# Summing the expert bias rows on 8 partitions, and lending their buffer to an eleventh Toeplitz slot

## The chip, the cores and the metric
The program runs on one core of one Trainium2 chip. The metric is the device time of the whole program in microseconds (us), the median of several runs. The kernel is written by hand for each engine: TensorE (PE in the profile), VectorE (DVE), ScalarE (ACT), GpSimd (POOL), and SyncE (SP), which issues most of the DMAs. Every engine runs its own list of instructions in order, and semaphores tie the lists together.

## The reference, cut to what matters
4096 tokens (32 sequences of 128) go through one layer with 256 channels:

```python
h = embed(ids)                                   # four tables, each with a projection to 256
n = layernorm(h)
x = silu(depthwise_conv(n @ w1.T + w1_b))
# state space: 16 states a channel, h = h * sigmoid(A) + x * B ; y = h . C + D * x, along one axis of x
y = ssm(x)
h = h + (y * silu(n @ v1.T + v1_b)) @ w2.T + w2_b
f = layernorm(h)
shared = silu(f @ sw1 + sb1) * (f @ sw3 + sb3) @ sw2 + sb2
# each token goes to two of eight experts, given by its number alone (11 n + 7919 k) mod 8
out = h + (shared + (expert_a(f) + expert_b(f)) / 2) / 2
```

An expert's second product adds its row `b2[e]` (256 numbers). A token of residue class e therefore ends with the constant row `0.5 * sb2 + 0.25 * (b2[e] + b2[e - 1])`, the same on all 128 partitions. There are 8 such rows, and they are what the change computes in another way.

## The kernel before, in words
**Phase A**, from the start to about 122 us, goes over four groups of 8 rows of 128 tokens (`run_phase_a`; the order of tasks in a row is `phase_a`). Per row, POOL gathers embeddings 6 rows ahead, TensorE transposes and projects them, ACT and DVE evacuate each product as a high and a low half, and the row is normalised: DVE `eps` (L1093), POOL `power_pair` (L613, one power -0.5 for two rows), DVE `norm` (L1079). Every finished row is stored by `h_store` (L471 to L475). Between its gathers POOL computes the state kernel (`kernel_step`), writes it to DRAM (L669) and then does `piece_lo(0)` (L675), the low half of a weight, at the head of group 3 (`group`, L677 to L690).

**The state stage**, from about 122 to 150 us, is 16 chunks of 16 channels. Chunk q takes 32 small matmuls (L1344 and L1346) against a Toeplitz matrix that SP loads in two DMAs (`toep_part`, `toep_load`) from the kernel rows in DRAM. The matrices lie in a ring of 10 slots of 8 KB a partition (`TRING`). Chunks 0 to 9 are loaded ahead, in phase A; chunks 10 to 15 are loaded into a slot when the chunk that used it is done (L538 to L540). A slot that is loaded again needs three quarters of the bytes, because its zero corner is there already. From chunk 8 on, each chunk is followed by four transposes (`y_turn`, L1326). ACT and DVE evacuate each half chunk (L918, L1151).

**Behind it** come the product with `w2`, the second layernorm, and eight expert slots of about 31 us each, in which TensorE works without gaps. The first bias row is needed in `mixer_1` (L763), where POOL adds it to the residual (L748).

**The bias rows before.** SP loads `sb2` and the eight rows `b2` to all 128 partitions after row 7 of group 0 (L504, L505). ACT scales them in rows 4 to 7 of group 1 (L848 to L853). POOL waits for half a chunk of the state stage (L712) and then adds them up with 17 chained instructions of 128x256 (L713 to L717). `w2_b` comes to all partitions twice: into `first_row` after all of the Toeplitz loads (L543), and into `w2_bias` when POOL's chain is done (L562).

**SP's order at the end of the stage** is: the reloads of chunks 10 to 15; `first_row`; the first quarter of the residual (`h_load(0, 0)`, L558); three weight pieces (L559); `w2_bias`; and after the last chunk four weight pieces, a residual part, and piece 8 (L563 to L568).

Of the kernel before, what the change touches and what calls it, by code (L numbers as in the profile page):

```python
# [15 lines left out]
F32 = mybir.dt.float32  # L16
# [26 lines left out]
TRING = TRIGHT + TLEFT  # L43
# [52 lines left out]
def _tower(nc, ctx, ids, table, small, rows, w_a, w_b, w_e, kernel_rows, h_rows, out):  # L96
# [6 lines left out]

    R, L = "right", "left"
    v_sb = sb(ctx, "v_sb", [P, HALVES, BATCH * SEQ], F32, R)
    w2_hi = sb(ctx, "w2_hi", [P, HALVES, D], F32R, R)
    w2_lo = sb(ctx, "w2_lo", [P, HALVES, D], F32R, R)
    bias_e = sb(ctx, "bias_e", [P, RES, D], F32, R)
# [43 lines left out]
    x_sil = sb(mem_a, "x_sil", [P, 4, 4, SEQ], F32, L)  # L152
    x_ids = sb(mem_a, "x_ids", [P, GROUPS, RES], I32, L)
# [18 lines left out]
    mem_row = ExitStack()  # L172
    first_row = sb(mem_row, "first_row", [P, 1, D], F32, L)
    mem_row.close()
# [27 lines left out]
    first_row_in = sem("first_row_in")  # L202
# [12 lines left out]
    bias_step = sem("bias_step")  # L215
# [180 lines left out]
    BIAS_STEPS = 1 + 2 * RES  # L396

# [19 lines left out]
    def toep(q):  # L417
        slot = q % TRING
        return toep_r[:, slot, :, :, :, :] if slot < TRIGHT else toep_l[:, slot - TRIGHT, :, :, :, :]
# [47 lines left out]
    def _(sp):  # L467
# [25 lines left out]

        def piece_in(n):
            raw, _, _, signal, _, _, _, src = PIECES[n]
            sp.dma_start(raw, src).then_inc(signal, 16)
# [7 lines left out]
        sp.dma_start(bias_row[:, 0:1, :], bass.AP(rows.tensor, D, [[0, P], [D, 1], [1, D]])).then_inc(rows_in, 16)  # L504
        sp.dma_start(bias_e[:, :, :], bass.AP(rows.tensor, 2 * D, [[0, P], [D, RES], [1, D]])).then_inc(rows_in, 16)  # L505
        for i in range(1, GROUPS - 1):
            for r in range(RES):
                h_store(i, r)
        last = GROUPS - 1
# [27 lines left out]
        toep_load(9)  # L537
        for q in range(TRING, NQ):  # L538
            sp.wait_ge(ssm_done, 2 * (q - TRING + 1))
            toep_load(q)  # L540
            if q == NQ - 1:
                sp.wait_ge(mm_done, 8 * GROUPS)
                sp.dma_start(first_row[:, :, :], bass.AP(rows.tensor, 0, [[0, P], [D, 1], [1, D]])).then_inc(first_row_in, 16)  # L543
# [13 lines left out]
        sp.wait_ge(ssm_done, 2 * (TRING - 3))  # L557
        h_load(0, 0)  # L558
        for n in range(1, 4):  # L559
            piece_in(n)  # L560
        sp.wait_ge(bias_step, BIAS_STEPS)
        sp.dma_start(w2_bias, bass.AP(rows.tensor, 0, [[0, P], [D, 1], [1, D]])).then_inc(rows_in, 16)  # L562
# [5 lines left out]
        piece_in(8)  # L568
        sp.wait_ge(h2_done, GROUPS)
# [20 lines left out]
    def _(pool):  # L590
# [86 lines left out]
        def group(i):  # L677

            for r in range(RES):
                if i == GROUPS - 1 and r == 0:  # L680
                    piece_lo(0)
                if r % 2 == 0 and (r or i):
                    power_pair(RES * i + r - 2, (r - 2) % 4)
                if r + LEAD < RES:
                    gather(i, r + LEAD)
                elif i + 1 < GROUPS:
                    gather(i + 1, r + LEAD - RES)
                if i == 1 and r or i == 2:
                    kernel_step(2 * (RES * (i - 1) + r) - 2)
                    kernel_step(2 * (RES * (i - 1) + r) - 1)  # L690
# [11 lines left out]

        steps = 0

        def link(ins):
            nonlocal steps
            steps += 1
            ins.then_inc(bias_step, 1)
            pool.wait_ge(bias_step, steps)

        pool.wait_ge(bias_scaled, 5)
        pool.wait_ge(ssm_done, 1)  # L712
        link(nc.gpsimd.tensor_copy(bias_row[:, 1, :], bias_e[:, RES - 1, :]))  # L713
        for e in range(RES - 1, -1, -1):
            before = bias_e[:, e - 1, :] if e else bias_row[:, 1, :]
            link(nc.gpsimd.tensor_tensor(bias_e[:, e, :], bias_e[:, e, :], before, ALU.add))
            link(nc.gpsimd.tensor_tensor(bias_e[:, e, :], bias_e[:, e, :], bias_row[:, 0, :], ALU.add))  # L717
        assert steps == BIAS_STEPS

# [31 lines left out]
        def mixer_1():  # L751
# [10 lines left out]
            power_step(GROUPS + 1, 1, eps2_done, rstd2_done)  # L762
            mixer_bias(0, 0, 0)  # L763
# [26 lines left out]
        def add_w2_bias(par, times, g, row=w2_bias):  # L790
# [4 lines left out]
            nc.gpsimd.tensor_tensor(at, at, row[:, 0, :], ALU.add).then_inc(h_biased, 1)  # L795
# [12 lines left out]
        pool.wait_ge(first_row_in, 16)  # L808
        for g in range(GROUPS):
            add_w2_bias(0, 1, g, first_row)  # L810
# [6 lines left out]
        pool.wait_ge(rows_in, 48)  # L817
# [10 lines left out]
    def _(act):  # L828
# [12 lines left out]
        def cat_hi(i, r):  # L841
# [6 lines left out]
            if isinstance(i, int) and i == 1 and r >= 4:  # L848
                if r == 4:
                    act.wait_ge(rows_in, 32)  # L850
                    nc.scalar.mul(bias_row[:, 0, :], bias_row[:, 0, :], 0.5).then_inc(bias_scaled, 1)
                at = bias_e[:, 2 * r - 8:2 * r - 6, :]
                nc.scalar.mul(at, at, 0.25).then_inc(bias_scaled, 1)  # L853
                if r == RES - 1:
                    piece_hi(0)
# [135 lines left out]
    def _(dve):  # L991
# [65 lines left out]
        def cat_lo(i, r):  # L1057
# [4 lines left out]
            if isinstance(i, int) and i == 0:  # L1062
                beside_cat(r)

# [467 lines left out]
```

## Time and profile before
| | |
|---|---|
| median of 3 runs | 422.75 us (422.54 to 425.06) |
| the profiled execution | 423.13 us, of which the span is 421.4 us |
| granted TensorE clock over the span | 0.996 |
| TensorE busy | 398.5 us, 95% of the span |
| weight loads on TensorE | 351.0 us, 83% |
| DVE, ACT, POOL busy | 271.0, 242.8 and 219.8 us |
| DMA | 39.01 MB, 93 GB/s over the span |
| DMA between 90 and 122 us | 309 GB/s, all 16 engines busy |

Busy time tells how long an engine had an instruction in it. TensorE's share is that of a pipelined engine, so the chain of waits and the engine's gaps tell more than the 95%. "Issue" as the cause of a gap means that the profile shows nothing that the engine waited for. Times in the rows are microseconds from the span's start.

### The profile page before, as it was taken

Reading aid. Unit: us, or ns where it says so; the run is one execution under the profiler, and the core shown is the slowest. Engines: PE = TensorE matmul, PEld = TensorE weight load, DVE = VectorE, ACT = ScalarE, POOL = GpSimd, SP = SyncE. Lnnn points to the kernel's source line nnn. Section 1 sums busy time; section 2 is a strip of 40 time slices with the busy share of each in tenths; the row PEclk is TensorE's granted clock in tenths of the full one; section 3 lists DMA queues with packets and bytes.
Section 4 is the critical chain, followed back from the end, with each engine's and each line's share of the span. In section 5 each row is a group of like instructions: output and inputs, shape, how many; then the busy total and the mean of one; then the engine's idle time right before and its main releaser. Section 6 shows DMA issues by size and latency. Waiting matters only on the chain.

```text
span 421.4 us, 8449 instructions
## 1 busy us (share of the span) xinstructions
PE 398.5 (95%) x2895; PEld 351.0 (83%) x2895; DVE 271.0 (64%) x609; ACT 242.8 (58%) x438; POOL 219.8 (52%) x265
## 2 busy tenths in 40 slices
PE   2899999999999898999999999999999999999996
PEld 1888887879778876888988988888888888888886
DVE  6887988879766698975564564554554554554333
ACT  4688978768886356635536536536436436436442
POOL 7788999821028084996346446446446446434000
PEclk9999999999999899999999999999999999999999
DMA  4353111299969971101301301301301301100101
GB/s 114 115 151 109 51 54 54 72 301 312 318 189 267 256 275 57 51 0 52 101 0 51 100 2 51 100 0 50 100 1 50 100 0 50 50 0 0 51 0 51
DMA packets 32924, 39.01 MB, mean 93 GB/s; under 512 B 3477, under 2 KB 29171, under 8 KB 32768
## 3 DMA queue, kind: packets, MB, share of 16 engines
q1 hardware_dynamic: 29760, 33.12, 26.1%
q0 software_dynamic: 3136, 5.52, 4.4%
q8 instruction: 16, 0.26, 0.3%
q14 instruction: 12, 0.10, 0.1%
HBM read 34.69 MB, written 8.65 MB: 103 GB/s over the span
## 4 chain that ended last, share of the span: by engine, by line
PE 74%; DVE 13%; issue 4%; ACT 4%; POOL 2%; DMA 1%; DVEq 0%; ACTq 0%; POOLq 0%
PE ps L1256 22%; PE ps L1258 21%; PE ps L1257 21%; PE ps L1344 3%; PE ps L1388 2%; DVE v_sb L1145 1%; DVE sw_lo L1136 1%; PE ps L1264 1%; DVE stat L1066 1%; PE ps L1297 1%; PE ps L1346 1%; DVE catT_lo L1059 1%; DVE x_mid L1120 1%; PE ps L1326 1%; DVE x_mid L1127 1%
## 5 line engine op out<-in xcount | busy, mean ns | idle before, releaser
L1193 DVE SCALAR_TENSOR_TENSOR hid_lo<-act_out,hid_hi 128x512 fp32r<-128x512 f32 x64 | 48.7, 763 | 55.9 <-ACT hid_hi L952 55.9
L939 ACT ACTIVATE act_out<-ps,vec 128x512 f32<-128x512 f32 x32 | 22.1, 690 | 89.5 <-PE ps L1258 89.5
L1187 DVE SCALAR_TENSOR_TENSOR act_out<-ps,vec,act_out 128x512 f32<-128x512 f32 x32 | 24.0, 750 | 50.7 <-ACT act_out L939 50.7
L748 POOL TENSOR_TENSOR h_sb<-h_sb,bias_e 128x256 f32<-128x256 f32 x32 | 24.5, 770 | 60.8 <-DVE h2n L1079 60.8
L1256 PE MATMUL ps<-h2nT_hi,sw_hi 128*128 128x512 f32 x128 | 50.0, 391 | 0.0
L1257 PE MATMUL ps<-h2nT_lo,sw_hi 128*128 128x512 f32 x128 | 50.0, 391 | 0.0
L1258 PE MATMUL ps<-h2nT_hi,sw_lo 128*128 128x512 f32 x128 | 50.0, 391 | 0.0
L741 POOL TENSOR_TENSOR zc_lo<-v_sb,zc_hi 128x256 fp32r<-128x256 f32 x32 | 29.8, 931 | 26.3 <-ACT zc_hi L929 26.3
L943 ACT ACTIVATE act_out<-ps,vec 128x512 f32<-128x512 f32 x32 | 22.1, 691 | 34.1 <-PE ps L1258 33.9
L606 POOL DMA_INDIRECT cat<-table_dram,x_ids x32 | 36.5, 1142 | 8.5 <-issue 6.2
L952 ACT ACTIVATE hid_hi<-act_out 128x512 fp32r<-128x512 f32 x64 | 39.7, 623 | 0.0
L1256 PE MATMUL ps<-sw_hi,hid_hi 128*128 128x256 f32 x128 | 37.9, 296 | 0.1
L1256 PE MATMUL ps<-ex_hi,hid_hi 128*128 128x256 f32 x128 | 36.9, 288 | 0.4 <-DVE hid_lo L1193 0.4
L1258 PE MATMUL ps<-ex_hi,hid_lo 128*128 128x256 f32 x128 | 36.2, 283 | 0.0
L1257 PE MATMUL ps<-ex_lo,hid_hi 128*128 128x256 f32 x128 | 36.2, 283 | 0.0
L1258 PE MATMUL ps<-sw_hi,hid_lo 128*128 128x256 f32 x128 | 36.1, 282 | 0.0
L1257 PE MATMUL ps<-sw_lo,hid_hi 128*128 128x256 f32 x128 | 36.1, 282 | 0.0
L1256 PE MATMUL ps<-proj_hi,catT_hi 128*128 128x256 f32 x96 | 30.4, 317 | 2.6 <-DVE catT_lo L1059 2.3
L1256 PE MATMUL ps<-hnT,wv_hi 128*128 128x512 f32 (+1 forms) x64 | 27.6, 431 | 1.0 <-ACT x_pad L897 0.5
L1258 PEld LDWEIGHTS ps<-h2nT_hi,sw_lo 128*128 128x128 f32 x128 | 24.0, 188 | 5.1
L1256 PEld LDWEIGHTS ps<-h2nT_hi,sw_hi 128*128 128x128 f32 x128 | 24.2, 189 | 4.1
L1258 PE MATMUL ps<-proj_hi,catT_lo 128*128 128x256 f32 x96 | 27.5, 286 | 0.0
(136 smaller groups left out, 1262.8 us busy)
## 6 DMA issues: line engine op xcount, KB each, us to landing
toep_l<-kernel_rows_dram SPq DMA_DIRECT2D x14, 512.0 KB, 7.3
toep_r<-kernel_rows_dram SPq DMA_DIRECT2D x12, 512.0 KB, 7.4
h_rows_dram<-h_ring SPq DMA_DIRECT2D x32, 128.0 KB, 2.1
h_in<-h_rows_dram SPq DMA_DIRECT2D x8, 512.0 KB, 4.4
stage<-w_e_dram POOLq DMA_DIRECT2D x7, 512.0 KB, 3.6
out_dram<-o_sb SPq DMA_DIRECT2D x7, 512.0 KB, 3.2
bias_e<-rows_dram SPq DMA_DIRECT2D x1, 1024.0 KB
toep_r<-kernel_rows_dram SPq DMA_DIRECT2D x4, 256.0 KB, 6.1
```

The source lines that it names most:

```text
L606: pool.indirect_dma_start(cat[:, r, :], None, table, bass.IndirectOffsetOnAxis(ap=x_ids[:, i, r:r + 1], axis=0), bounds_check=VOCAB - 1, o ...
L741: nc.gpsimd.tensor_tensor(zc_lo[:, g, :, :], z_cols(e, g), f32(zc_hi[:, g, :, :]), ALU.subtract).then_inc(zc_lo_done, 1)
L748: nc.gpsimd.tensor_tensor(at, at, bias_e[:, bass.ds(e, 1), :].rearrange("p o c -> p (o c)"), ALU.add).then_inc(h2_biased, 1)
L939: nc.scalar.activation(act_out[:, n % 4, :], ps[bank][:, :], ACT.Silu, bias=vec[:, C_SB1 + j:C_SB1 + j + 1]).then_inc(act_done, 1)
L943: nc.scalar.activation(act_out[:, n % 4, :], ps[bank][:, :], ACT.Gelu, bias=vec[:, bass.ds(C_B1 + 2 * x + j, 1)]).then_inc(act_done, 1)
L952: nc.scalar.mul(hid_hi[:, n % 4, :], act_out[:, n % 4, :], 0.5 if kind == SHARED else 0.25).then_inc(hid_hi_done, 1)
L1187: nc.vector.scalar_tensor_tensor(act_out[:, n % 4, :], ps[bank + 1][:, :], vec[:, C_SB3 + j:C_SB3 + j + 1], act_out[:, n % 4, :], ALU.add, ...
L1193: nc.vector.scalar_tensor_tensor(hid_lo[:, n % 4, :], act_out[:, n % 4, :], 0.5 if kind == SHARED else 0.25, f32(hid_hi[:, n % 4, :]), ALU ...
L1256: nc.tensor.matmul(out_, hi, rhs_hi, start=start, stop=False, **kw)
L1257: nc.tensor.matmul(out_, hi, rhs_lo, start=False, stop=False, **kw)
L1258: return nc.tensor.matmul(out_, lo, rhs_hi, start=False, stop=stop, **kw)
L1344: nc.tensor.matmul(at, t_hi, x_sb[:, c, :, :].rearrange("u w b -> u (w b)"), start=True, stop=False, skip_group_check=True)
```

## The change
- The ring gets an eleventh slot, `toep_b`, at the address of `bias_e`, which is 8 KB a partition as well. The upper left half of the slot is cleared by POOL in group 3, behind `piece_lo(0)`; its chunk 10 is then loaded with the bytes of a reload, behind chunk 9. Chunks 11 to 15 are reloads. A reload of chunk q now waits for chunk q - 11.
- `sb2` (8 times) and the rows `b2` (once as they are, once shifted by one) are loaded to 8 partitions, in a part of `x_sil` that group 1 does not use yet: four small DMAs in group 1 (`bias_part`). DVE adds them in rows 5 and 6, ACT scales the sum in row 7 (one 8x256 instruction in place of one 128x256 and four 128x512), and SP stores the 8 rows to DRAM.
- `bias_e` is loaded from there to all partitions behind piece 8, after the state stage. POOL waits for it ahead of the first use.
- POOL's 17 instructions, `first_row` and its load, and the later load of `w2_bias` are gone; `w2_bias` is loaded once, in group 1.
- SP loads the first residual part right after its wait for chunk 6, and then waits for all projections ahead of pieces 1 to 3.

```diff
-TRING = TRIGHT + TLEFT
+TRING = TRIGHT + TLEFT + 1
...
+    mem_b = ExitStack()
+    toep_b = sb(mem_b, "toep_b", [P, PAIRS, SEQ, 2, 2], F16, R)
+    mem_b.close()
     bias_e = sb(ctx, "bias_e", [P, RES, D], F32, R)
...
+    b2_at, b2_before = x_sil[0:RES, 3, 0:2, :], x_sil[0:RES, 3, 2:4, :]
+    sb2_rows, bias_rows = x_sil[0:RES, 2, 0:2, :], x_sil[0:RES, 2, 2:4, :]
...
-        sp.dma_start(bias_row[:, 0:1, :], bass.AP(rows.tensor, D, [[0, P], [D, 1], [1, D]])).then_inc(rows_in, 16)
-        sp.dma_start(bias_e[:, :, :], bass.AP(rows.tensor, 2 * D, [[0, P], [D, RES], [1, D]])).then_inc(rows_in, 16)
+        half = [SEQ, 2], [1, SEQ]
         for i in range(1, GROUPS - 1):
             for r in range(RES):
                 h_store(i, r)
+                if i == 1 and r == 0:
+                    bias_part(b2_at, bass.AP(rows.tensor, 2 * D, [[D, RES], *half]))
+                    bias_part(b2_before[1:RES], bass.AP(rows.tensor, 2 * D, [[D, RES - 1], *half]))
+                if i == 1 and r == 1:
+                    bias_part(b2_before[0:1], bass.AP(rows.tensor, (RES + 1) * D, [[D, 1], *half]))
+                    bias_part(sb2_rows, bass.AP(rows.tensor, D, [[0, RES], *half]))
+                if i == 1 and r == 2:
+                    sp.dma_start(w2_bias, bass.AP(rows.tensor, 0, [[0, P], [D, 1], [1, D]])).then_inc(rows_in, 16)
+            if i == 1:
+                sp.wait_ge(bias_scaled, 1)
+                sp.dma_start(h_bias, bias_row[0:RES, 1, :]).then_inc(bias_out, 16)
...
         toep_load(9)
+        sp.wait_ge(top_zero, 1)
+        toep_part(TRING - 1, 0, HALF)
+        toep_part(TRING - 1, 1, 0)
         for q in range(TRING, NQ):
             sp.wait_ge(ssm_done, 2 * (q - TRING + 1))
             toep_load(q)
-            if q == NQ - 1:
-                sp.wait_ge(mm_done, 8 * GROUPS)
-                sp.dma_start(first_row[:, :, :], bass.AP(rows.tensor, 0, [[0, P], [D, 1], [1, D]])).then_inc(first_row_in, 16)
...
-        sp.wait_ge(ssm_done, 2 * (TRING - 3))
+        sp.wait_ge(ssm_done, 2 * 7)
         h_load(0, 0)
+        sp.wait_ge(mm_done, 8 * GROUPS)
         for n in range(1, 4):
             piece_in(n)
-        sp.wait_ge(bias_step, BIAS_STEPS)
-        sp.dma_start(w2_bias, bass.AP(rows.tensor, 0, [[0, P], [D, 1], [1, D]])).then_inc(rows_in, 16)
...
         piece_in(8)
+        sp.wait_ge(bias_out, 16)
+        sp.dma_start(bias_e[:, :, :], bass.AP(h_bias.tensor, 0, [[0, P], [D, RES], [1, D]])).then_inc(bias_in, 16)
...
                 if i == GROUPS - 1 and r == 0:
                     piece_lo(0)
+                    nc.gpsimd.memset(toep_b[:, :, 0:HALF, :, :].rearrange("p j t c w -> p j (t c w)").bitcast(F32),
+                                     0.0).then_inc(top_zero, 1)
...
-        pool.wait_ge(bias_scaled, 5)
-        pool.wait_ge(ssm_done, 1)
-        link(nc.gpsimd.tensor_copy(bias_row[:, 1, :], bias_e[:, RES - 1, :]))
-        for e in range(RES - 1, -1, -1):
-            before = bias_e[:, e - 1, :] if e else bias_row[:, 1, :]
-            link(nc.gpsimd.tensor_tensor(bias_e[:, e, :], bias_e[:, e, :], before, ALU.add))
-            link(nc.gpsimd.tensor_tensor(bias_e[:, e, :], bias_e[:, e, :], bias_row[:, 0, :], ALU.add))
...
+            pool.wait_ge(bias_in, 16)
             mixer_bias(0, 0, 0)
...
-        pool.wait_ge(first_row_in, 16)
+        pool.wait_ge(rows_in, 16)
         for g in range(GROUPS):
-            add_w2_bias(0, 1, g, first_row)
+            add_w2_bias(0, 1, g)
...
             if isinstance(i, int) and i == 1 and r >= 4:
-                if r == 4:
-                    act.wait_ge(rows_in, 32)
-                    nc.scalar.mul(bias_row[:, 0, :], bias_row[:, 0, :], 0.5).then_inc(bias_scaled, 1)
-                at = bias_e[:, 2 * r - 8:2 * r - 6, :]
-                nc.scalar.mul(at, at, 0.25).then_inc(bias_scaled, 1)
+                if r == 7:
+                    act.wait_ge(bias_summed, 2)
+                    nc.scalar.mul(bias_row[0:RES, 1, :].rearrange("p (b t) -> p b t", b=2), bias_rows, 0.5).then_inc(bias_scaled, 1)
...
+            if isinstance(i, int) and i == 1 and r == 5:
+                dve.wait_ge(bias_parts_in, 64)
+                nc.vector.tensor_tensor(b2_at, b2_at, b2_before, ALU.add).then_inc(bias_summed, 1)
+            if isinstance(i, int) and i == 1 and r == 6:
+                dve.wait_ge(bias_summed, 1)
+                nc.vector.scalar_tensor_tensor(bias_rows, b2_at, 0.5, sb2_rows, ALU.mult, ALU.add).then_inc(bias_summed, 1)
```

## Rows read from the trace of the kernel before

**Rows 1.** Chain that ended last, by engine, from the page
```profile
PE 74%; DVE 13%; issue 4%; ACT 4%; POOL 2%; DMA 1%; DVEq 0%; ACTq 0%; POOLq 0%
```
**Rows 2.** TensorE in order of time, chunks 11 to 15: start, us, line, idle before
```profile
139.66 0.19 PE L1344 MATMUL ps<-x_sb,toep_r 128*128 128x64 f16 x1
...
142.31 0.18 PE L1346 MATMUL ps<-x_sb,toep_r 128*128 128x32 f16 x1 [1.45 <-issue]
...
143.19 0.26 PE L1344 MATMUL ps<-x_sb,toep_r 128*128 128x64 f16 x1
...
147.03 0.19 PE L1344 MATMUL ps<-x_sb,toep_l 128*128 128x64 f16 x1
...
148.56 0.19 PE L1344 MATMUL ps<-x_sb,toep_l 128*128 128x64 f16 x1
```
**Rows 3.** Busy us by stretch: PE, PEld, DVE, ACT, POOL, granted clock, DMA share, GB/s
```profile
90.00:103.00 13.00, 13.00 (x90) 11.77 (x89) 10.92 (x26) 10.73 (x21) 1.81 (x2) 1.00 1.04 336
121.50:124.90 3.40, 3.21 (x65) 2.79 (x64) 0.74 (x3) 1.97 (x5) 1.70 (x3) 1.00 0.06 19
125.00:138.00 13.00, 12.84 (x287) 11.83 (x285) 8.38 (x21) 8.47 (x23) 10.45 (x15) 1.00 1.00 252
142.40:145.80 3.40, 3.40 (x51) 3.28 (x51) 2.13 (x5) 1.12 (x3) 0.00 (x0) 0.50 1.04 289
```
**Rows 4.** DMA queues between 139.3 and 141.2 us: kind, packets, MB, engine share
```profile
q8 instruction: 1, 0.02, 5.5%
q14 instruction: 1, 0.01, 1.1%
```
**Rows 5.** Issue at 136.06 us of the last reload: size, us to landing
```profile
toep_l<-kernel_rows_dram SPq DMA_DIRECT2D x1, 512.0 KB, 10.7
```
**Rows 6.** POOL in order of time: start clear, and around the head of group 3
```profile
1.07 0.97 POOL L594 MEMSET x_pad<- 128x1040 f32 x1
...
81.19 1.32 POOL L675 TENSOR_TENSOR w_lo<-toep_r,w_hi 128x512 fp32r<-128x512 f32 x1
82.44 0.74 POOL L613 TENSOR_TENSOR rstd<-rstd,minus_half 128x2 f32<-128x2 f32 x1
```
**Rows 7.** DVE and TensorE in order of time, behind that power
```profile
83.22 0.80 DVE L1079 TENSOR_SCALAR hn<-h_ring,mv,rstd 128x256 f32<-128x256 f32 x2 [1.47 <-POOL rstd L613]
...
87.24 0.39 PE L1256 MATMUL ps<-proj_hi,catT_hi 128*128 128x256 f32 x1 [0.74 <-DVE catT_lo L1059]
```
**Rows 8.** Chain of waits in group 1: start, us, what
```profile
34.32 0.42 ACT bias_row L851
34.74 0.52 ACT bias_e L853
...
44.80 0.60 DVE x_sb L1114
```
**Rows 9.** DVE in order of time: half-width prices, and one beside POOL's work
```profile
41.45 0.72 DVE L1120 SCALAR_TENSOR_TENSOR x_mid<-x_pad,vec,x_mid 128x512 f32<-128x512 f32 x1
42.20 0.98 DVE L1127 SCALAR_TENSOR_TENSOR x_mid<-x_pad,vec,x_mid 128x512 f32<-128x512 f32 x1
```
**Rows 10.** POOL in order of time: bias chain's first, residual, split, first bias
```profile
123.04 0.40 POOL L713 COPY bias_row<-bias_e 128x256 f32<-128x256 f32 x1 [15.66 <-PE ps L1346]
...
148.48 2.81 POOL L795 TENSOR_TENSOR h_in<-h_in,first_row 128x256 f32<-128x256 f32 x4 [11.94 <-DMA h_in<-h_rows_dram]
...
153.83 0.88 POOL L741 TENSOR_TENSOR zc_lo<-v_sb,zc_hi 128x256 fp32r<-128x256 f32 x1
...
178.92 1.26 POOL L748 TENSOR_TENSOR h_sb<-h_sb,bias_e 128x256 f32<-128x256 f32 x1
```
**Rows 11.** SP's queue in order of time: reloads and what follows, piece 8
```profile
123.45 7.29 SPq L487 DMA_DIRECT2D toep_r<-kernel_rows_dram  x8
130.79 6.72 SPq L487 DMA_DIRECT2D toep_l<-kernel_rows_dram  x4
...
153.79 0.33 SPq L496 DMA_DIRECT2D stage<-w_e_dram  x1
```

More of the change, by code:

```diff
@@ L101, in sb @@
         return stack.enter_context(nc.sbuf_tensor(name, shape, dt, side=side))
+    h_bias = nc.dram_tensor("bias_rows_dram", (RES, D), F32, kind="Internal").ap()
     R, L = "right", "left"
@@ L171, in _tower @@
     ex1_hi = sb(ctx, "ex1_hi", [P, 2, BLK], F32R, L)
-    mem_row = ExitStack()
-    first_row = sb(mem_row, "first_row", [P, 1, D], F32, L)
-    mem_row.close()
     ex1_lo = sb(ctx, "ex1_lo", [P, 2, BLK], F32R, L)
@@ L201, in _tower @@
     rows_in = sem("rows_in")
-    first_row_in = sem("first_row_in")
+    bias_parts_in = sem("bias_parts_in")
+    bias_out = sem("bias_out")
+    bias_in = sem("bias_in")
+    top_zero = sem("top_zero")
     ident_step = sem("ident_step")
@@ L214, in _tower @@
     bias_scaled = sem("bias_scaled")
-    bias_step = sem("bias_step")
+    bias_summed = sem("bias_summed")
     cat_zero = sem("cat_zero")
@@ L394, in _tower @@
     K_FIRST = 1 + 2 * 5 + 1
-    BIAS_STEPS = 1 + 2 * RES
     def hn_bank():
@@ L418, in toep @@
         slot = q % TRING
+        if slot == TRING - 1:
+            return toep_b[:, :, :, :, :]
         return toep_r[:, slot, :, :, :, :] if slot < TRIGHT else toep_l[:, slot - TRIGHT, :, :, :, :]
@@ L492, in toep_load, with bias_part @@
             toep_part(q, 1, 0)
+        def bias_part(dst, src):
+            sp.dma_start(dst, src).then_inc(bias_parts_in, 16)
         def piece_in(n):
@@ L700, in _ @@
         power_pair(RES * GROUPS - 2, (RES - 2) % 4)
[L703 to L709, printed above, removed]
-        pool.wait_ge(bias_scaled, 5)
-        pool.wait_ge(ssm_done, 1)
-        link(nc.gpsimd.tensor_copy(bias_row[:, 1, :], bias_e[:, RES - 1, :]))
-        for e in range(RES - 1, -1, -1):
-            before = bias_e[:, e - 1, :] if e else bias_row[:, 1, :]
-            link(nc.gpsimd.tensor_tensor(bias_e[:, e, :], bias_e[:, e, :], before, ALU.add))
-            link(nc.gpsimd.tensor_tensor(bias_e[:, e, :], bias_e[:, e, :], bias_row[:, 0, :], ALU.add))
-        assert steps == BIAS_STEPS
         def expert_in(n, par):
@@ L788, in mixer, with add_w2_bias @@
                     add_w2_bias(1 - par, times, 2 * g - 3)
-        def add_w2_bias(par, times, g, row=w2_bias):
+        def add_w2_bias(par, times, g):
             if g == 0:
@@ L794, in add_w2_bias @@
             at = h_in[:, par, g, :]
-            nc.gpsimd.tensor_tensor(at, at, row[:, 0, :], ALU.add).then_inc(h_biased, 1)
+            nc.gpsimd.tensor_tensor(at, at, w2_bias[:, 0, :], ALU.add).then_inc(h_biased, 1)
         def slot(e, par, times, load=True, bias=True):
@@ L816, in _ @@
             power_step(g, g, eps2_done, rstd2_done)
-        pool.wait_ge(rows_in, 48)
         pool.wait_ge(h2n_done, GROUPS)
```

## Prediction
> **What bounds the kernel now.** I read the chain of waits first. Of its steps 74% are TensorE's [rows 1], so a step elsewhere costs time only where TensorE is made to stand. I then went through TensorE in order of time, looking for its gaps near the parts that the change touches. There are three such places.
>
> The first is the end of the state stage. At full pace a chunk with its four transposes takes 148.56 - 147.03 = 1.53 us. From chunk 11 to chunk 14 three such steps should take 4.59 us, and they took 147.03 - 139.66 = 7.37 us: 2.78 us are lost [rows 2]. The loss has two parts. TensorE stood still inside chunk 11 for 1.45 us, with nothing to wait for that the profile shows [rows 2], and behind that its granted clock was 0.50 (1.2 GHz) for 3.4 us, where it had been 1.00 [rows 3]. Around the gap the DMA queues moved two packets of kind "instruction" between 139.3 and 141.2 us, one of them of 0.02 MB that took 5.5% of 16 engines' 1.9 us, so one engine's for 1.7 us [rows 4]. So I read the gap as code that came late through DMA engines that were busy: the transfers run at 1.00 of their time from 125 to 138 us, at 252 GB/s [rows 3]. The matrices themselves are not late. The last one is issued at 136.06, lands 10.7 us later at 146.8 [rows 5], and is used at 148.56 [rows 2]: 1.8 us to spare.
>
> The second place is the head of group 3. POOL's power ends at 83.2 [rows 6]; DVE stood 1.47 us for it, and TensorE 0.74 us for DVE [rows 7]. From 90 to 103 us TensorE is busy for 13.00 of 13.00 us [rows 3], so it doesn't win back what it loses there.
>
> The third is group 1, where ACT's scaling of the bias rows (0.42 and 0.52 us) stands in the chain at 34.3 us, and where the chain then runs through DVE until 45.4 [rows 8].
>
> **The change, part by part.** *POOL's clear of the new slot.* It covers 1024 floats a partition, and stands between `piece_lo(0)` and the power for which DVE and TensorE wait [rows 6, 7]. The nearest row is the clear of 1040 floats, 0.97 us [rows 6], so this one takes 1024 / 1040 of it, 0.95 us. Nothing hides it: POOL goes from 81.19 into the power without a gap [rows 6]. **+0.95 us**, between 0 (if another wait takes its place) and 1.2.
>
> *Group 1.* The two ACT instructions leave the chain: -0.94 us [rows 8]. The three others that go from ACT lie beside the DVE stretch and bring nothing, and the new one in row 7, at most the 0.42 us of the old one, lies there too. DVE gets two instructions of 256 columns in that stretch, at half of 0.72 us each: +0.75 with rounding [rows 9]. One 512-column instruction of the same kind took 0.98 instead, so the upper bound is 2 x 0.49 = 1.0 us [rows 9]. Together **-0.2 us**, between -0.9 (the DVE pair falls into a gap) and +0.1. The small loads start a whole group row or more before DVE reads them. SP's wait for ACT's row 7 comes behind a store that needs the same row, and holds nothing up. The 1 MB load that leaves this stretch had nobody waiting for it.
>
> *The eleventh slot.* Chunk 10 is now loaded behind chunk 9, ahead of the stage. The engines have room for its 768 KB: from 121.5 to 124.9 us they were used for 0.06 of the time [rows 3]. Five reloads of 768 KB follow in place of six. The reloads are issued from 123.45 to 137.5 [rows 11], and each stands for about 2.3 to 3.3 us of transfer, so the last matrix should land some 3 us sooner in the stage. That was not late, so by itself it brings **0**. It matters only if TensorE's 2.78 us go away: chunk 15 would then start at 145.8, a microsecond before its matrix used to land [rows 2, 5].
>
> *Does the gap go?* Here I had to choose. Code that came late must have been asked for earlier, and what it met is the queue of about 130 to 139 us, where a transfer took up to 10.7 us to land [rows 5]. The first five reloads after the change are issued at the same points of the stage, and are the same size, as the first five before (chunks 0 to 4 free their slots, as now). Only what is sixth differs: it is among the last of the 12 issues that end at 137.5 [rows 11], and the residual and the weights take its place. So the fetch meets the same backlog, and I take the gap and the slow clock to **stay**: 0. The ends are -2.78 (both go) and +2.78 (another such gap).
>
> The Trainium skill (Runtime: NRT & Kernel Launch, "Instruction fetch mechanics") says that each engine fetches its next 16 KiB of code on a queue of its own while it runs the current one, and that crossing such a block is mostly hidden. By that rule the gap isn't code and the queue has no say in it, so that only the other terms would be left, the same +0.75. The two packets and the gap at the same place [rows 2, 4] speak against "hidden", and I keep a third of the chance for a gap that hangs on the transfers and goes.
>
> *POOL's chain.* The 17 instructions start at 123.04 and are over long before POOL's next work; POOL then stood 11.94 us for the residual until 148.48 [rows 10]. Taking them away brings 0. The residual now comes ahead of `first_row`, and one reload sooner, some 3 us. POOL's additions and its weight half end at 153.8, just as its first split of the mixer starts [rows 10], so if the stage ends sooner POOL doesn't hold it up. If the stage doesn't end sooner, ACT's input sets that split, and 0 is won. SP's new wait for all projections ends at about 135, before SP gets there; behind it are only the three weight pieces.
>
> *The load of the sums.* 1 MB is issued behind piece 8, at about 154.2 [rows 11]. At the 252 GB/s of the stage it takes 4 us, with the 10.7 us of a full queue it lands by 165 [rows 3, 5]. POOL first reads it at 178.92 [rows 10]: 14 us to spare. Queued behind POOL's wait are its splits and residual additions, none of them due earlier. SP issues one load more ahead of its wait for the residual of slot 2, about 0.5 us, and isn't late.
>
> **The sum.** +0.95 - 0.2 + 0 = +0.75 us on the profiled execution's 423.13 (span 421.4 and 1.7 around it), 423.9. That execution lies 0.4 above the median, so the median should go from 422.75 to **423.5 us**. With the terms' own bounds: 421.8 to 424.1.
>
> **The rivals.** *The gap goes.* The fetch's turn is a matter of a microsecond: had it come 1.45 us sooner, there would be no gap and no slow clock. One reload less in the stage, and 128 KB less ahead of the residual, speak for it; the same backlog at 135 us speaks against. Then 423.5 - 2.8 = **420.7 us**, down to 419.3 with the best of the other terms.
>
> *Slower: a second gap.* The extra 768 KB close the pause at 122 us, so that the engines go into the stage with work queued, and code fetches there wait longer. It decides if one more fetch is late by the microseconds that this one was. For it: the engines run full from 125 on [rows 3]. Against: the extra load should be through by 125, and the total is the same. Price: one more gap with its half clock, 2.8 us: **426.3 us**, and 427 with the clear at its upper bound.
>
> *The clear costs nothing.* If another wait, such as that for the embeddings' transposes, covers it, +0.95 falls away: **422.5 us**. For it: the chain runs through many short waits there. Against: rows 7.
>
> *The change doesn't do what it says*, and the loads stay in the old order: SP has to wait for the clear, at 84 us, and is only at chunk 1 then. I see no way to that.
>
> **How the numbers follow.** Forecast 0.45, gap gone 0.32, second gap 0.13, clear hidden 0.10. A measurement of this kernel can tell about 1%, 4.2 us, from no change; that is below 418.5 or above 427.0. Neither the forecast nor a rival's middle reaches these. From the rival of the gap gone I give 0.04 to faster, from the second gap 0.05 to slower, and the rest, 0.91, to within 1%. The range of 8 in 10 takes in the forecast's own range and most of the gap gone, and leaves out the second gap and the last tenths of the other end: 419.8 to 425.8.
>
> **What would show it.** The clear: DVE's wait for POOL at 83 us grows from 1.47 to about 2.4 us, and TensorE's gap behind it from 0.74 to 1.7. Group 1: no bias instruction of ACT in the chain, and DVE's last step there within half a microsecond of 45.4. The slot: transfers also between 121.5 and 124.9, and the last matrix landed about 21 us after the stage's first matmul, not 24.6. The gap: one of about 1.5 us without a named cause in chunks 9 to 13, and a stretch at clock 0.50 behind it. If the stage takes 25 us and not 27.6, the forecast is wrong and the first rival right. What would make it wrong elsewhere is a wait on the sums at 179 us, or slower code fetches of ACT and DVE while the sums are loaded.

## The result and the profile after

The changed kernel takes **424.38 us** in the median of 22 runs (422.97 to 426.42), the kernel before, run beside it, 422.23 us (421.29 to 425.5, 22 runs). The ratio is 1.0037, with a 95% interval of 1.0021 to 1.0053: slower by 1.6 us (0.9 to 2.2), which is clear of the noise and under 1%. The medians themselves are 2.15 us apart. The profiled execution has a span of 422.5 us, 1.1 above the span of before.

*The head of group 3.* POOL and DVE in order of time, in the profile after (start, us, line, idle before with its releaser):

```profile
81.14 1.31 POOL L695 TENSOR_TENSOR w_lo<-toep_r,w_hi 128x512 fp32r<-128x512 f32 x1
82.38 0.97 POOL L702 MEMSET toep_b<- 128x1024 f32 x1
83.29 0.73 POOL L633 TENSOR_TENSOR rstd<-rstd,minus_half 128x2 f32<-128x2 f32 x1
```
```profile
84.06 0.80 DVE L1088 TENSOR_SCALAR hn<-h_ring,mv,rstd 128x256 f32<-128x256 f32 x2 [2.34 <-POOL rstd L633]
```

TensorE in the same stretch:

```profile
84.98 0.66 PE L1293 MATMUL ps<-ident,hn 128*128 128x128 f32 x4 [0.86 <-DVE hn L1088]
...
88.09 0.39 PE L1265 MATMUL ps<-proj_hi,catT_hi 128*128 128x256 f32 x1 [0.73 <-DVE catT_lo L1062]
```

They answer [rows 6, 7]. The power starts at 83.29, where it started at 82.44. DVE's wait for it grew from 1.47 to 2.34 us. TensorE has its old gap of 0.73 and a new one of 0.86 ahead of it. From the start of POOL's split (L695) to the start of the power it now takes 2.15 us, where it took 1.25. The stage's first matmul comes at 123.03 us, 0.85 later than before (122.18); the line of before and that of after:

```profile
122.18 0.22 PE L1344 MATMUL ps<-x_sb,toep_r 128*128 128x64 f16 x1 [0.19 <-DVE x_sb L1114]
```
```profile
123.03 0.22 PE L1353 MATMUL ps<-x_sb,toep_r 128*128 128x64 f16 x1 [0.20 <-DVE x_sb L1123]
```

*The state stage.* TensorE in order of time, to be held against [rows 2]:

```profile
140.48 0.19 PE L1353 MATMUL ps<-x_sb,toep_r 128*128 128x64 f16 x1
...
143.54 0.18 PE L1355 MATMUL ps<-x_sb,toep_r 128*128 128x32 f16 x1 [1.89 <-issue]
...
144.46 0.26 PE L1353 MATMUL ps<-x_sb,toep_r 128*128 128x64 f16 x1
...
148.24 0.19 PE L1353 MATMUL ps<-x_sb,toep_r 128*128 128x64 f16 x1
```

The gap without a named cause is there again, in chunk 11, in front of the same matmul of the program (the stage's last of that chunk). It is 1.89 us, not 1.45. From its first to its last matmul the stage takes 27.76 us, where it took 27.41. Stretches of the profile after, with the columns of [rows 3]:

```profile
121.50:124.90 3.40, 3.20 (x45) 2.63 (x44) 1.43 (x3) 2.28 (x4) 0.00 (x0) 1.00 0.92 270
125.00:138.00 13.00, 12.85 (x292) 11.88 (x291) 8.29 (x20) 8.53 (x22) 0.00 (x0) 1.00 0.93 233
143.30:146.70 3.40, 3.15 (x42) 3.03 (x42) 1.76 (x4) 1.12 (x3) 0.65 (x1) 0.50 0.95 373
```

The pause in the transfers is filled (0.92 where the share was 0.06), and the stretch at clock 0.50 is there, 3.4 us long as before. DMA queues from 140.2 to 142.3 us (kind, packets, MB, share of 16 engines):

```profile
q1 hardware_dynamic: 505, 0.45, 96.0%
q8 instruction: 1, 0.02, 5.9%
```

The instruction packet takes 5.9% of 16 engines' 2.1 us, so 1.98 us of one engine; in [rows 4] it was 1.7.

Not every execution has the stretch at clock 0.50. It lasts 3.4 us, so it takes about 0.004 off the granted clock of a span of 422 us; the profiles that show it have 0.994 to 0.996 over the span, those that don't have 1.000. Of the changed kernel's 22 runs, 8 have 0.998 or more (median 423.48 us) and 14 have 0.996 or less (424.7). Of 53 runs of the kernel before that were made later, beside the experiments, 29 have 0.998 or more (422.24) and 24 have 0.996 or less (423.7); one more run, at 641.59 us and a clock of 0.56, is left out everywhere. So the changed kernel is slower by 1.2 us among the runs without the stretch and by 1.0 among those with it. That it has the stretch in 14 of 22 runs and not in 24 of 53 can be chance. The two profiles show one execution each, both of the kind with the stretch; no trace of these two kernels shows how long the gap is in the other kind.

In the profile after, the last reload is issued at 134.0 and lands 10.6 us later:

```profile
toep_l<-kernel_rows_dram SPq DMA_DIRECT2D x1, 512.0 KB, 10.6
```

That is 144.6, 21.6 us after the stage's first matmul; before it was 24.6. POOL in order of time, which answers [rows 10]:

```profile
146.05 2.82 POOL L801 TENSOR_TENSOR h_in<-h_in,bias_row 128x256 f32<-128x256 f32 x4 [37.83 <-DMA h_in<-h_rows_dram]
152.47 2.37 POOL L695 TENSOR_TENSOR ex_lo<-stage,ex_hi 128x1024 fp32r<-128x1024 f32 x1 [3.60 <-ACT ex_hi L844]
...
180.08 1.25 POOL L753 TENSOR_TENSOR h_sb<-h_sb,bias_e 128x256 f32<-128x256 f32 x1
```

The 17 bias instructions are gone, and the residual comes 2.4 us earlier. The first bias addition doesn't wait for the sums.

*Group 1.* Chain of waits (start, us, what):

```profile
34.00 0.58 ACT x_pad L900
34.58 0.37 ACT h_ring L869
...
38.90 0.32 DVE x_sil L1069
...
43.07 0.60 DVE x_sil L1072
...
44.43 0.59 DVE x_sb L1123
```

ACT's bias rows have left the chain (0.94 us), and the two DVE instructions stand in it for 0.92 us, so the exchange by itself is worth nothing. DVE's `x_sb` starts 0.37 us earlier than in [rows 8], but by TensorE's matmuls 0.29 us of lead stood at 21 us already, before SP issues the first of the new loads at 26.9 us. And the lead doesn't last. In group 2 one DVE instruction takes nearly twice its time beside a pair of POOL's:

```profile
70.55 1.44 DVE L1136 SCALAR_TENSOR_TENSOR x_mid<-x_pad,vec,x_mid 128x512 f32<-128x512 f32 x1
```
```profile
70.69 1.89 POOL L658 TENSOR_TENSOR toep_r<-toep_r 128x256 f32<-128x256 f32 x2
```

TensorE then stands for DVE:

```profile
72.51 0.39 PE L1265 MATMUL ps<-proj_hi,catT_hi 128*128 128x256 f32 x1 [1.16 <-DVE catT_lo L1062]
```

In the trace before, the same DVE instruction took 0.75 us, with POOL busy until 71.71 on a gather's DMA, and there was no such gap:

```profile
70.84 0.75 DVE L1127 SCALAR_TENSOR_TENSOR x_mid<-x_pad,vec,x_mid 128x512 f32<-128x512 f32 x1
```

At the head of group 3 TensorE is 0.05 us behind the kernel before.

So the two profiled executions account for the span's difference of 1.1 us like this: +0.05 up to group 3, +0.80 through the clear (0.85 at the stage), +0.35 in the stage, -0.1 behind it. The interval of the measured change (0.9 to 2.2 us) holds that sum. Part of the rest lies outside the span: measured time less span is 1.94 us in the mean of the 22 runs, and 1.72 in the 53 of the kernel before.

### The profile page after: what moved, and what is told of

It reads as the page before. It is cut to its first block, busy times and chain, and to the rows that moved or that the text cites. A ratio compares the mean times of both kernels' runs of the same rounds, so it can differ in the third digit from the quotient of the medians.

```text
span 422.5 us, 8434 instructions
## 1 busy us (share of the span) xinstructions
PE 398.9 (94%) x2895; PEld 351.7 (83%) x2895; DVE 272.1 (64%) x611; ACT 241.2 (57%) x434; POOL 207.2 (49%) x249
## 4 chain that ended last, share of the span: by engine, by line
PE 72%; DVE 15%; issue 5%; ACT 3%; POOL 3%; DMA 1%; DVEq 0%; POOLq 0%; ACTq 0%
PE ps L1265 21%; PE ps L1266 21%; PE ps L1267 21%; PE ps L1353 3%; PE ps L1397 2%; DVE x_mid L1129 1%; DVE catT_lo L1062 1%; DVE stat L1075 1%; DVE hn L1088 1%; DVE v_sb L1154 1%; DVE sw_lo L1145 1%; PE ps L1355 1%; PE ps L1273 1%; PE ps L1335 1%; PE ps L1306 1%
## 5 line engine op out<-in xcount | busy, mean ns | idle before, releaser
L801 POOL TENSOR_TENSOR h_in<-h_in,bias_row 128x256 f32<-128x256 f32 x32 | 25.2, 810 | 37.8 <-DMA h_in<-h_rows_dram 37.8
L746 POOL TENSOR_TENSOR zc_lo<-v_sb,zc_hi 128x256 fp32r<-128x256 f32 x32 | 29.7, 927 | 26.9 <-ACT zc_hi L932 26.9
```

Source lines behind the costliest of these rows:

```text
L746: nc.gpsimd.tensor_tensor(zc_lo[:, g, :, :], z_cols(e, g), f32(zc_hi[:, g, :, :]), ALU.subtract).then_inc(zc_lo_done, 1)
L801: nc.gpsimd.tensor_tensor(at, at, w2_bias[:, 0, :], ALU.add).then_inc(h_biased, 1)
```

## The experiments

The theory: the clear costs what it takes; the gap is code that came late behind queued transfers, and it stays because the backlog stays. The rivals: the slot's load or its wait makes the difference, or the gap is TensorE's own and the transfers have no say in it. Each kernel is the changed one with an edit, but for the last, which is the kernel before with one. Ratios are to the kernel before, run beside it; the two kernels with shifted code have one run each and no ratio.

**The clear, late.** POOL clears the slot two powers later, in row 3 of group 3.

```
 for r in range(RES):
     if i == GROUPS - 1 and r == 0:
         piece_lo(0)
-        nc.gpsimd.memset(toep_b[...], 0.0).then_inc(top_zero, 1)
+    if i == GROUPS - 1 and r == 3:
+        nc.gpsimd.memset(toep_b[...], 0.0).then_inc(top_zero, 1)
```

> The changed kernel with one edit: POOL clears the new slot in row 3 of group 3 and not in row 0, where it then stands idle for 2 us for DVE's next row. Theory (the clear stands in the chain through POOL's power): DVE's wait for POOL at 83 us goes back from 2.34 to about 1.5 us, the state stage starts 0.85 us sooner than in the changed kernel, and the time is about 0.85 us below the changed kernel's, so about 0.7 us above the kernel before. Rival (the clear only took the place of another wait, and the loss lies in the state stage): no change against the changed kernel, about 1.6 us above the kernel before.

Measured: 423.47 us (12 runs), ratio 1.0004 (0.9984 to 1.0025). DVE at the head of group 3, and POOL's clear in its new place:

```profile
83.40 0.73 DVE L1089 TENSOR_SCALAR hn<-h_ring,mv,rstd 128x256 f32<-128x256 f32 x2 [1.17 <-POOL rstd L633]
```
```profile
88.98 0.94 POOL L703 MEMSET toep_b<- 128x1024 f32 x1
```

DVE's wait for POOL is half of what it was. The stage starts at 122.29, 0.74 us earlier than in the changed kernel; the gap is the same 1.89 us. By the traces the clear costs about 0.75 us of TensorE's time where it stands, and next to nothing two powers later (122.29 against the 122.18 of before). The other traces agree on the mechanism: from the start of POOL's split to the start of the power it takes 2.15 or 2.16 us in the changed kernel and in the four kernels below that clear at the same place (no reloads, two in flight, 4 and 16 shifted), and 1.25 or 1.26 in the five traces without a clear there. By the measured times alone the late clear can't be told from the changed kernel, since their intervals touch (0.9984 to 1.0025, and 1.0021 to 1.0053).

**No reloads.** The loop that loads chunks 11 to 15 is left out, and TensorE waits for the first load of each slot alone. This leaves out the matrices of five chunks: they multiply by what lies in the slots.

```
-for q in range(TRING, NQ):
-    sp.wait_ge(ssm_done, 2 * (q - TRING + 1))
-    toep_load(q)
...
-loads = q // TRING
+loads = 0
```

> The changed kernel without the five reloads of chunks 11 to 15: TensorE multiplies by what is in the slots, so the work of TensorE stays the same and 3.8 MB of transfers in the state stage are left out. Theory (TensorE's gap is code that comes late through busy DMA engines): no gap of over 0.5 us in chunk 11 or elsewhere in the stage, no stretch at half clock, the stage 3.2 us shorter than the changed kernel's (27.9 to about 24.7 us from the first matmul of chunk 0 to the last of chunk 15), and the whole about 3.2 us below the changed kernel's, 1.6 below the kernel before. Rival (the gap is something of TensorE's own list of instructions at that place, whatever the transfers do): the gap of 1.5 to 1.9 us stays at the end of chunk 11, and the clock falls behind it.

Measured: 420.89 us (10 runs), ratio 0.9950 (0.9926 to 0.9974). Stretches from 125 on:

```profile
125.00:138.00 13.00, 12.84 (x295) 11.88 (x294) 8.29 (x20) 8.52 (x23) 0.80 (x2) 1.00 0.28 91
140.00:150.00 10.00, 9.56 (x199) 9.33 (x197) 9.34 (x20) 5.04 (x12) 0.88 (x2) 1.00 0.18 53
```

With the transfers at a share of 0.28 there is no gap and no half clock, and the stage takes 24.60 us. All 10 runs have a granted clock of 0.998 or more. The gap hangs on the transfers: 27.76 - 24.60 = 3.2 us of the changed kernel's stage.

**Two reloads in flight.** This keeps every transfer and only takes the depth out of the queue: ahead of each reload SP waits until the one two before it has landed. A reload is two DMAs.

```
+def landed(q):
+    sp.wait_ge(toep_in[q % TRING], 32 * (1 + q // TRING))
 for q in range(TRING, NQ):
     sp.wait_ge(ssm_done, 2 * (q - TRING + 1))
+    landed(q - 2)
     toep_load(q)
...
+landed(NQ - 2)
 h_load(0, 0)
 sp.wait_ge(mm_done, 8 * GROUPS)
+landed(NQ - 1)
```

> The changed kernel with SP waiting, ahead of each reload, until the reload two before it has landed (and so for the residual and the weight pieces behind them), so that at most two loads are queued. The bytes are the same. Theory A (the fetch of code waits behind the backlog of queued transfers): the gap in chunk 11 shrinks below 0.7 us or goes, with the half clock, and the time falls by 2 to 3 us against the changed kernel. Theory B (the fetch waits for its turn with engines that are busy, whatever is queued behind): the gap stays at 1.5 to 2 us and the time stays within 0.5 us of the changed kernel's. If the pacing makes the matrices late, TensorE's gaps are instead ahead of a chunk.

Measured: 421.42 us (12 runs), ratio 0.9964 (0.9948 to 0.9980). Stretches, and TensorE at the matmul in front of which the gap was:

```profile
125.00:138.00 13.00, 12.84 (x292) 11.85 (x290) 8.29 (x20) 8.53 (x22) 0.00 (x0) 1.00 0.92 235
140.00:150.00 10.00, 9.20 (x197) 8.89 (x195) 8.82 (x20) 5.15 (x13) 2.96 (x5) 1.00 0.80 229
```
```profile
142.08 0.18 PE L1361 MATMUL ps<-x_sb,toep_r 128*128 128x32 f16 x1 [0.36 <-issue]
```

The engines are used as much from 125 to 138 (0.92 at 235 GB/s; the changed kernel has 0.93 at 233), and yet 0.36 us of the gap is left and the clock stays at 1.00 (2.4 GHz), in all 12 runs at 0.998 or more. The stage takes 25.13 us, and the time is 3.0 us below the changed kernel's, where theory A had 2 to 3. It is also 2.1 us below the 423.48 of the changed kernel's runs without a stretch at half clock, so those too lose something that the pacing removes. So it isn't the bandwidth in use that delays the code, it is what has been issued ahead of it. The same shows in the 3.9 us in which the fetch waits (see the table of fetches below): first the changed kernel, then this one, then the kernel with both edits, which has no gap at all.

```profile
136.33:140.23 3.90, 3.90 (x98) 3.90 (x95) 2.44 (x6) 2.19 (x7) 0.00 (x0) 1.00 1.05 244
136.37:140.27 3.90, 3.90 (x98) 3.90 (x96) 2.43 (x6) 2.19 (x7) 0.00 (x0) 1.00 0.90 234
134.67:138.57 3.90, 3.90 (x98) 3.90 (x96) 2.41 (x6) 2.19 (x7) 0.00 (x0) 1.00 1.03 224
```

**The code shifted.** Matmuls of 2 columns at TensorE's start move all its later code: 16 of them, and 4 in a second kernel. Each is counted as two in the trace (the 16 stand as x32).

```
+for _ in range(16):
+    nc.tensor.matmul(MM[1][:, 0:2], ident[:, :], ident[:, 0:2], start=True, stop=True)
```

> The changed kernel with 16 matmuls of 2 columns more on TensorE at the very start, into a bank that is not yet used, where TensorE stands idle for the first embeddings. All of TensorE's later code is so moved by 32 instructions. Theory (the gap is where a block of code ends): the gap moves 16 matmuls ahead, from the last matmul of chunk 11 to the last of that chunk's first half, and keeps its size within 0.7 us. Rival (the gap belongs to a semaphore, a bank or a load of chunk 11): it stays at the last matmul of chunk 11.

> The changed kernel with 4 matmuls of 2 columns more on TensorE at the very start, which the trace counts as 8 since they are in fp32 and take two passes; the run with 16 of them showed the same and cost 5 us at the start, so these cost about 1 us there. Theory (the gap stands at the end of a block of code): counted over all matmuls from the start, the gap stays at the same place as in the kernel before and the changed kernel, at the 1099th, or a whole block of some 125 away from it; counted within the stage it so comes 8 matmuls sooner, at the 375th and not the 383rd. Rival: it stays at the 383rd of the stage, the last of chunk 11.

One run each: 429.49 us with 16 (they cost 5 us at the start by themselves), 423.85 with 4. TensorE at the gap, with 16 and then with 4:

```profile
140.68 0.21 PE L1355 MATMUL ps<-x_sb,toep_l 128*128 128x64 f16 x1 [1.66 <-issue]
```
```profile
142.76 0.22 PE L1355 MATMUL ps<-x_sb,toep_r 128*128 128x64 f16 x1 [1.85 <-issue]
```

Counted from zero over the matmuls of the trace from the program's start, the gap stands in front of matmul number 1099 in the kernels before and after, 1100 with the 4, and 974 with the 16. With 4 it keeps its number in the program to within one, and so moves seven matmuls towards the stage's start, from number 383 to 376 (the stage's matmuls without its transposes, counted from zero). That is a place in the code, not in the work. With 16 the expected place in chunk 11 was wrong: the gap went 125 numbers towards the start, into chunk 7. I read 974 and 1099 as the ends of two blocks of code that follow each other, of one instruction packet each (0.02 MB in the trace). In the changed kernel number 974 comes behind a pause that TensorE makes anyway at the end of chunk 7 (2.54 us from its start to that of chunk 8, 1.07 for the chunk before): its fetch ended at 134.64, and TensorE got there at 136.34. With 16 shifted it falls ahead of that pause, and the fetch is late.

The fetches themselves, from the trace's DMA records (us; the first column counts from the stage's first matmul):

```
kernel                 fetch starts  took  ended at  TensorE resumes  idle
before                     17.22     1.68   141.08       142.31       1.45
changed                    17.25     1.99   142.26       143.54       1.89
clear late                 18.00     1.19   141.48       142.81       1.89
ring of ten (below)        17.29     1.85   141.33       142.56       1.73
4 shifted                  17.89     1.08   141.49       142.76       1.85
16 shifted                  9.91     1.29   139.12       140.68       1.66
two in flight              16.20     1.29   140.55       142.08       0.36
before, paced (below)      15.12     1.07   138.60         -            0
both edits (below)         14.28     0.93   136.58         -            0
no reloads                 13.38     0.94   137.22         -            0
```

In five kernels with the gap at this place TensorE goes on 1.23 to 1.33 us behind the end of the fetch, whenever that is, and 1.5 behind it in two more. Without the reloads the fetch starts 3.9 us earlier and takes half the time. With the gap's fixed number in the code, that shows the gap to be the wait for code.

The table also shows where the time goes. TensorE comes to number 974, the end of the block before, 13.3 us into the stage in all of these kernels whose code isn't shifted. Without the reloads the fetch starts 0.1 us behind that; with both edits 1.0 us, in the kernel before with pacing 1.8, with two in flight 2.9, and with the deep queue 3.9 to 4.7. So if the fetch is asked for at that place, which the trace doesn't record, most of the delay lies ahead of the packet's start, and the packet's own 0.9 to 2.0 us is the smaller part.

**A ring of ten.** The changed kernel's bias rows with the old ten slots: no clear, no slot, six reloads.

```
-TRING = TRIGHT + TLEFT + 1
+TRING = TRIGHT + TLEFT
...
-sp.wait_ge(top_zero, 1)
-toep_part(TRING - 1, 0, HALF)
-toep_part(TRING - 1, 1, 0)
```

> The changed kernel with a ring of ten slots again: no eleventh slot, no clear by POOL, chunk 10 as a reload in the stage; the bias rows stay as in the change. Theory (the loss of the change is the clear, plus a gap for late code that the slot makes no better; the new way of the bias rows is neutral): the stage starts at 122.2 to 122.4 us, the gap of 1.5 to 1.9 us stays in chunk 11, and the time lies within 0.5 us of the kernel before. Rival (the new way of the bias rows itself costs, by DVE's two instructions in group 1 or by the load behind the stage): it stays 0.7 us or more above the kernel before.

Measured: 423.46 us (12 runs), ratio 1.0016 (0.9997 to 1.0035); the gap is 1.73 us at the same matmul, the stage takes 27.60 and starts at 122.19, as before. By the ratio it is 0.7 us above the kernel before, by the medians 0.9, which is outside the theory's 0.5 and at the rival's 0.7. The interval (-0.1 to +1.5 us) holds both, so whether the new way of the bias rows costs something stays open; the trace shows no loss up to the stage's start. The intervals of this kernel and of the one with the late clear overlap too: with the queue left deep, the slot itself is worth nothing that can be measured. What the traces show clearly of the changed kernel's 1.6 us is the clear at its place.

**Both edits.** The late clear and the two in flight together.

> The changed kernel with both edits that helped: the clear in row 3 of group 3, and at most two loads queued in the stage. Theory (the two losses are apart and add): 0.85 to 1.4 us below the paced kernel, so about 420.3 us, 2.2 to 2.9 us below the kernel before (ratio about 0.994), with the clock at 1.00 throughout and no gap over 0.7 us from 82 to 150 us. Rival (a later start of the stage hid something, such as matrices that land late): no more than 0.3 us below the paced kernel, with a gap ahead of a chunk.

Measured: 420.46 us (8 runs), ratio 0.9951 (0.9922 to 0.9980): 2.1 us below the kernel before (422.53 beside it), the lowest median of the kernels that do all of the work, and near the expected 420.3; from the two in flight alone it can't be told. The stage takes 24.64 us from 121.37, as without reloads. It starts 0.92 us earlier than with the late clear alone; in this execution POOL starts its split at 80.45 us, where it starts at 81.38 with the late clear alone. No experiment says why, and nothing shows that the edits are the cause. TensorE's first wait behind the stage is short:

```profile
152.16 0.38 PE L1272 MATMUL ps<-w_hi,zc_hi 128*128 128x256 f32 x1 [0.81 <-POOL zc_lo L753]
```

**The kernel before, paced.** The same three waits in the kernel before, with its ten slots. The question is whether the slot is worth something once the gap is gone.

> The kernel before, ring of ten, with the same pacing: each reload waits until the one two before it has landed, and so do the residual and the weights. Theory (a short queue is what lets the code in, the eleventh slot isn't needed for it): the gap in chunk 11 shrinks below 0.7 us, and the time falls by 1.5 to 3 us. Rival (with six reloads to pace, the last matrix or the residual comes late): a gap of TensorE ahead of chunk 15 or a late start behind the stage, and a gain below 1 us.

Measured: 424.9 us (12 runs), ratio 1.0052 (1.0029 to 1.0076): slower by 2.2 us where the theory had 1.5 to 3 us faster, though the gap in chunk 11 is gone as it said and the stage takes 25.11 us. The loss is the rival's late start behind the stage. TensorE, POOL, ACT and the stretch behind it:

```profile
156.59 0.39 PE L1261 MATMUL ps<-w_hi,zc_hi 128*128 128x256 f32 x1 [3.73 <-POOL zc_lo L746]
```
```profile
148.15 2.79 POOL L800 TENSOR_TENSOR h_in<-h_in,first_row 128x256 f32<-128x256 f32 x4 [11.46 <-DMA h_in<-h_rows_dram]
153.36 2.36 POOL L680 TENSOR_TENSOR ex_lo<-stage,ex_hi 128x1024 fp32r<-128x1024 f32 x1 [2.41 <-ACT ex_hi L844]
```
```profile
152.17 1.05 ACT L844 CAST ex_hi<-stage 128x1024 fp32r<-128x1024 f32 x1 [4.07 <-DMA stage<-w_e_dram]
```
```profile
158.00:161.20 3.20, 3.20 (x17) 3.20 (x16) 3.00 (x12) 0.00 (x0) 2.10 (x4) 0.50 0.09 37
```

Six paced reloads push the first weights back. POOL takes up the residual at 148.15, which is not the loss: without pacing it was 148.48 [rows 10]. It then stands for ACT, and ACT stands 4.07 us for the weights. SP issues these at 146.43, where it issued them at 139.43 without pacing and issues them at 143.39 with both edits. So the mixer's first split is late, TensorE stands 3.73 us, and the clock falls to 0.50 (1.2 GHz) behind that. The gap went from the stage to the mixer. Ten of the 12 runs have such a stretch by their granted clock, and five of them (0.992) two.

The two paced kernels, which ran beside the same kernel before, are 4.4 us apart (424.9 and 420.46). By the traces it is the sixth reload that makes the difference: the last two reloads are issued at 135.69 and 139.69 here, and the fifth and last of the kernel with both edits at 136.39. But the two differ in the bias rows, in `first_row` ahead of the residual and in the clear as well, and a ring of ten with the new bias rows and the pacing wasn't run. That the slot alone is worth it is argued and not shown.

## Why the prediction was right

The forecast was 423.5 us, from +0.75; measured were 424.38, inside its range of 419.8 to 425.8, and its case was the right one. The size was under half of what came: the change is +1.6 us by the ratio and +2.15 by the medians, and both lie above the +1.3 of the forecast's own upper bounds (424.1). Luck helped the total: the forecast stood on a median of 3 runs, 422.75, and the median of 22 was 422.23, which hides 0.5 us of the miss in the change. Of what would show it, DVE's wait came out at 2.34 (about 2.4 forecast), TensorE's idle time behind the clear at 0.86 + 0.73 = 1.59 (1.7), and the stage at 27.76 us (27.6). Point by point:

- **The clear, +0.95.** Right. It took 0.97 us and moved POOL's power by 0.90, TensorE lost about 0.8 between group 3's head and the stage, and 0.74 came back when it was moved.
- **Group 1, -0.2.** The forecast was -0.2, and it was -0.38 at group 2's head, but that nearness is chance: the exchange in the chain was -0.94 + 0.92, and 0.29 us of the lead stood before the change had done anything. The pair of DVE instructions was priced at 0.75 and took 0.92. What I missed too is that the lead is not carried on: in group 2 it turned into +0.05, at the DVE instruction that ran beside POOL's pair. The term should have been 0, which is 0.2 us of the miss.
- **The eleventh slot, 0.** Right as far as this kernel goes. The last matrix landed 21.6 us after the stage's start where I expected about 21, and no one had waited for it. That it would count once the gap is gone I only named for chunk 15; in the paced kernels what comes late behind the sixth reload is the first weights, and it costs far more.
- **The gap stays, 0.** The mechanism was right, and the size was off. The gap is code that waits behind the backlog, the first five reloads are those of before, and the gap stood at the same matmul. But it was 0.43 us longer, and the stage 0.35; this is the term that was mis-sized. The fetch started at the same point of the stage (17.25 us, 17.22 before) and took 1.99 us, not 1.68. I had ends of -2.78 and +2.78 for this term and nothing between. The five kernels with the gap at this place put it at 1.45 to 1.89 us, all of the other four above the kernel before, so part of this can be chance of one execution; I can't tell how much. The 2.78 us that the forecast took as the kernel's loss are those of one execution too: 29 of the 53 runs of the kernel before had no stretch at half clock. In such runs the loss of the stage is smaller than the forecast took it, by how much no trace shows.
- **The rule of hidden crossings.** I gave the gap that hangs on transfers a third of the chance, and the row spoke against "hidden". The runs decide: of the Trainium skill (Runtime: NRT & Kernel Launch, "Instruction fetch mechanics") the queue of its own agrees with the trace (kind "instruction", 0.02 MB), and "mostly hidden" doesn't, at 1.45 to 1.89 us and the half clock behind it. The same section says that TensorE's code memory holds 128 KiB, eight such blocks. With TensorE going on 1.3 us behind each late fetch, and the fetch of the block at number 1099 starting only behind TensorE's passing of number 974, these traces show no such reserve.
- **POOL's chain and the load of the sums, 0 each.** Right. The residual came 2.4 us earlier and POOL then waited 3.60 us for ACT. The load of the sums was issued at 155.24 and landed at 162.6, where I had 165 as the latest, 17 us ahead of its use.
- **The other rivals.** The clear isn't hidden, and the gap didn't go by itself: it took pacing. The second gap had its place right: the engines did go into the stage full. No second fetch came late enough to be seen, though with the code shifted by 16 matmuls the block ahead did. Two of the rivals' ends are added up wrongly, without effect on the chances: a second gap with the clear at its upper bound is 426.6 and not 427, and the gap gone with the best of the other terms 419.0 and not 419.3.

The sum with the sizes of the two profiles is 0.05 + 0.80 + 0.35 - 0.1 = 1.1 us. The 0.5 us from there to the 1.6 of the ratio no experiment takes apart; the time outside the span, 0.2 us more in the mean, is part of it.

## What to carry to other kernels

A gap without a releaser on an engine with much code, with an instruction packet that ends about 1.3 us ahead of its end, was a wait for code here. Where you see one, look how many bytes are issued ahead of that packet, and let few bulk loads be in flight (two kept 235 GB/s here). Look first at what stands behind those loads in the same queue, since it is pushed back: pacing brought the changed kernel, with five reloads, to a ratio of 0.9964, and the kernel before, with six, to 1.0052. Look at the granted clock of all the runs and not only of the profiled one, since a stretch at half clock can be there in some and not in others. And a clear of a microsecond belongs at a point where no engine waits for the next thing on that queue.

## What the runs showed of the hardware

- **The queue and not the load delays a code fetch.** At like shares of the DMA engines (0.92 and 0.93) and like bandwidth (235 and 233 GB/s) the gap was 0.36 and 1.89 us; what differed was how much was issued ahead. With both edits it was 0, at a share of 1.03 in the stretch in which the fetch waits. The Trainium skill (DMA: Bandwidth & Descriptors, "Queues, rings and completion order") has the engines take turns between queues packet by packet. By that rule the depth of another queue would not matter to the fetch; here it does. The fetch of the block behind number 1099 started 0.1 us behind TensorE's passing of number 974 with no reloads, and 3.9 to 4.7 us behind it with the deep queue; what it waits for there no record shows.
- **The half clock lasts the same.** In the seven profiles with it, six behind a gap of 1.45 to 1.89 us in the stage and one behind the 3.73 us in the mixer, the granted clock is 0.50 for 3.41 us and then 1.00 again. Behind the idle times of 0.36 to 1.16 us shown above it stays at 1.00. These are single executions, and the granted clocks of the other runs say that 8 of 22 of the changed kernel had no such stretch.
- **A matmul of 2 columns in fp32 isn't cheap at the program's start.** The 32 that the trace counts for 16 of them took 6.99 us, 0.22 us each. Each comes with a weight load of its own of 128x128, which the trace gives 0.29 to 0.33 us, overlapping the next. What they cost later in a program no run shows.
